# A feed-forward block: the next block's transposes put ahead of the last row tile, and the router's softmax put eight groups behind its matmuls

## The reference

```python
x = x + layernorm(attention(layernorm(x), W_qkv, W_out))
x = x + layernorm(ffn(layernorm(x), router_w, w1, b1, w2, b2))

def ffn(x, router_w, w1, b1, w2, b2):
    xt = x.reshape(-1, H)                                 # H = 1024, F = 4096
    p = softmax(matmul(xt, router_w))                     # 8 experts
    top, idx = top_k(p, 2)
    top = top / sum(top)
    combine = einsum('tk,tke->te', top, one_hot(idx, 8))
    out = matmul(gelu(matmul(xt, w1) + b1), w2) + b2
    return out * sum(combine, axis=-1, keepdims=True)
```

## Time and profile before

| what | value |
|---|---|
| profiled execution, device time | 1846.83 us |
| its span (slowest core, core 6) | 1845.3 us |
| spans of the eight cores | 1804.3 to 1845.3 us |
| mean granted TensorE clock of the cores | 0.902 to 0.924 |
| runs listed | 1857.76 and 1940.99 us, median 1899.37 us |
| TensorE busy | 1445.2 us, 78% of the span |

### The profile page before, as it was taken

How to read it: one execution, slowest core, us unless ns; L and a number is a source line. 1 busy time by engine, 2 the same in 40 slices (tenths; PEclk the granted TensorE clock), 3 DMA queues, 4 the chain that set the end, 5 groups by cost and what they waited for, 6 DMA issues and landing times.

```text
span 1845.3 us, 19508 instructions; the slowest of 8 cores (1804.3 to 1845.3 us)
## 1 busy us (share of the span) xinstructions
PE 1445.2 (78%) x6816; PEld 648.8 (35%) x6816; DVE 594.8 (32%) x1102; ACT 558.7 (30%) x1181; POOL 57.9 (3%) x101
## 2 busy tenths in 40 slices
PE   0588777888788788878878888873897897897897
PEld 0233333333334333333333333331343343343343
DVE  0443444543233333333333333332213213214103
ACT  0402110220132233323333333334353353353333
POOL 1000000000000000000000000101000000000000
PEclk9989999899998888888888988887898898998898
DMA  9312201110400111111100001878703002102002
GB/s 137 64 29 46 46 12 35 23 23 1 86 7 1 29 29 29 29 29 28 22 24 26 19 28 29 125 143 144 119 24 83 10 24 70 22 13 79 1 1 80
DMA packets 51617, 81.55 MB, mean 44 GB/s; under 512 B 19648, under 2 KB 27840, under 8 KB 51520
## 3 DMA queue, kind: packets, MB, share of 16 engines
q0 software_dynamic: 27280, 50.35, 16.7%
q1 hardware_dynamic: 24240, 29.94, 5.3%
HBM read 97.08 MB, written 20.97 MB: 64 GB/s over the span
## 4 chain that ended last, share of the span: by engine, by line
PE 65%; DVE 13%; DMA 10%; issue 6%; ACT 3%; SPq 1%; DVEq 0%; POOL 0%; ACTq 0%; POOLq 0%
PE pAll L185 31%; PE pAll L160 31%; DMA qtile<-qs 5%; DMA xgb<-xo 3%; DVE ptb L750 2%; PE pAll L216 2%; DMA qs<-qstage 2%; DVE vt L496 2%; DVE xfg L439 1%; DVE sm L374 1%; DVE m L677 1%; DVE x2t L832 1%; DMA x2lt<-x2s 1%; DVE qstage L467 1%; PE pAll L1061 1%
## 5 line engine op out<-in xcount | busy, mean ns | idle before, releaser
L160 PE MATMUL pAll<-kf,qtile 128*128 128x512 bf16 x1024 | 256.8, 411 | 35.5 <-DMA qtile<-qs 32.1
L160 PE MATMUL pAll<-x2f,w1b 128*128 128x512 bf16 x1024 | 237.8, 396 | 24.3 <-ACT h1g L1162 20.1
L185 PE MATMUL pAll<-vt,ptb 128*128 128x512 bf16 x1024 | 226.4, 382 | 0.9 <-DVE ptb L750 0.9
L185 PE MATMUL pAll<-w2b,h1g 128*128 128x512 bf16 x1024 | 221.7, 379 | 4.1 <-ACT h1g L1162 4.1
L677 DVE TENSOR_REDUCE m<-pAll 128x1 f32<-128x512 f32 x128 | 88.5, 692 | 353.5 <-PE pAll L160 353.2
L160 PEld LDWEIGHTS pAll<-kf,qtile 128*128 128x128 bf16 x1024 | 106.0, 105 | 177.6 <-issue 80.2
L688 ACT ACTIVATE pbuf<-pAll,nb 128x512 bf16<-128x512 f32 x128 | 87.8, 686 | 261.1 <-DVE nb L682 261.1
L160 PEld LDWEIGHTS pAll<-x2f,w1b 128*128 128x128 bf16 x1024 | 102.9, 101 | 157.2 <-issue 47.7
L185 PEld LDWEIGHTS pAll<-vt,ptb 128*128 128x128 bf16 x1024 | 100.8, 98 | 123.9 <-issue 4.8
L185 PEld LDWEIGHTS pAll<-w2b,h1g 128*128 128x128 bf16 x1024 | 99.9, 98 | 125.9 <-issue 6.0
L185 PE MATMUL pAll<-wvb,xfg 128*128 128x512 bf16 x512 | 115.6, 379 | 35.5 <-DVE vt L496 35.5
(11 more groups left out here) (109 smaller groups left out, 1032.2 us busy)
## 6 DMA issues: line engine op xcount, KB each, us to landing
xrt<-xo POOLq DMA_DIRECT2D x16, 512.0 KB, 7.8
x2s<-x2t SPq DMA_DIRECT2D x16, 512.0 KB, 3.7
w1b<-w POOLq DMA_DIRECT2D x8, 1024.0 KB, 32.1
w2b<-w POOLq DMA_DIRECT2D x4, 2048.0 KB, 45.0
x2rt<-x2s SPq DMA_DIRECT2D x16, 512.0 KB, 5.3
y<-yt SPq DMA_DIRECT2D x16, 512.0 KB, 3.3
xgb<-xo POOLq DMA_DIRECT2D x16, 256.0 KB, 8.4
qs<-qstage POOLq DMA_DIRECT2D x16, 256.0 KB, 2.7
```

The source lines that it names most:

```text
L160: return e.matmul(o(), l(), r(), start=st, stop=sp)
L185: return e.matmul(o(), l(), r(), start=st, stop=sp)
```

## The change

`c_pass2` is cut in two. `c_pass2_mm`, behind fc = 6, keeps the router's matmuls and the four copies to `rt8`. `c_pass2_chain`, behind fc = 14, has the rest: maximum, Exp and the steps to `sc4`, tile after tile as before. And `c_pass1(gc + 1)` is called behind the epilogue of k = 2 instead of behind that of k = 3. What is computed stays the same. The lines behind L1084 are numbered differently in the changed kernel: L1100 is L1102, L1112 to L1140 are L1120 to L1148, L1162 is L1170, L1195 is L1205, L1208 is L1218, L1217 is L1227.

```diff
-    def c_pass2(gc):
+    ev_rtcp = {}
+
+    def c_pass2_mm(gc):
         for t in range(4):
-            qt = gc * 4 + t
             bank = rt_banks[t % 2]
...
             mm_group(bank, mms, waits=list(ev_x2f_evac[(gc, t)]) + [ev_rw])
             r8 = rt8[:, t * 8:(t + 1) * 8]
             wrt = list(rt_slice_prev.get(t, ()))
-            ev_rt = read_bank("scalar", [bank],
-                              lambda e, d=r8, b=bank: e.copy(d, b.ap[:, 0:8]),
-                              waits=wrt, inc="sS")
+            ev_rtcp[(gc, t)] = read_bank(
+                "scalar", [bank],
+                lambda e, d=r8, b=bank: e.copy(d, b.ap[:, 0:8]),
+                waits=wrt, inc="sS")
+
+    def c_pass2_chain(gc):
+        for t in range(4):
+            qt = gc * 4 + t
+            r8 = rt8[:, t * 8:(t + 1) * 8]
+            ev_rt = ev_rtcp[(gc, t)]
             mxr = rsm[:, 0:1]
...
             if fc == 6:
-                c_pass2(gc)
+                c_pass2_mm(gc)
+            elif fc == 14:
+                c_pass2_chain(gc)
         cx2f_free[0] = E.ev("tS")
...
-        if gc + 1 < 4:
-            c_pass1(gc + 1)
+            if k == 2 and gc + 1 < 4:
+                c_pass1(gc + 1)
```

## The result

The changed kernel took 1870.4 us (median of 11 runs), the kernel before 1847.1 (median of 10); the ratio is 1.0134, 95% interval 1.0088 to 1.0180. It is slower, by 1.3%.

A forecast was written before the change was run, and what follows sets the result against it. TensorE, busy for 78% of the span, was taken as the bound. The profiled 1846.8 us plus 21.7 for the move of c_pass1 and 2.8 for the router split gave 1871.3, stated as 1871 us; range 1857 to 1892.

The forecast's parts named there:

- the price of the clock: Lower granted clock slows matmuls behind each new GELU wait ahead of group 3: 2.7 us lost, bounds 0 and 2.9.
- The boundary: From copy of k = 2 to the next block's fourth up-projection group: 41.15 us against 36.6, so 4.55 later.
- The move alone: Moving c_pass1 behind k = 2's epilogue costs 7.2 us at each of three block boundaries, +21.7 (13.6 to 22.4).
- The router: Splitting the router pass: chain as long as before, router fills now outside it; +0.7 us four times, +2.8 (0 to 4).
- No cost at k = 3: The 64 matmuls of k = 3 behind c_pass1 run at full rate, 13.8 us; at half rate 13.8 more each.
- A clock that stays up: Rival: clock does not fall ahead of group 3 or behind the wait at fc = 14; 1847 us, chance 0.05.
- Longer table switches: Rival: seven new ScalarE table switches behind busy work last longer than their load; 1876 us, chance 0.08.
- The two others: Rivals: k = 3 stays at lower clock, 1912 us, 0.05; casts overtake the epilogue at boundaries, 1841 us, 0.02.
- within 2%: Whole kernel's time changes by less than about 2%, here 37 us; chance 0.89, slower by more 0.09, faster 0.02.

The follow-up runs named there:

- experiments 1 to 3: Stage (before 563.2 us): 1, split only 566.9, move only 580.9; 2, changed kernel, casts ahead of k = 2's epilogue, 553.2; 3, six up-projection banks, changed 546.4, before 535.8.
- Experiment 4: Changed kernel with matmuls whose result nothing reads, filling TensorE's GELU waits ahead of groups 3 and 18; stage 573.9 us against 585.7 for the changed kernel.
- experiment 7: Scratch columns per router tile, four Exp one behind the other: on the changed kernel, stage 541.5 us; on the kernel of experiment 6, 480.8.
- 504.8 kernel: Kernel before, router pass whole, with c_pass1 between matmuls and epilogue of k = 2 and six up-projection banks; stage 504.8 us against 563.2.
- experiment 6: 504.8 kernel with the four router fills in one bank, one copy of 32 columns, and seven up-projection banks; stage 502.4 us.

## Where the prediction was right, and the step that failed

The mechanism was right: each wait that was forecast appears where it was forecast, and the change costs 22.5 us for a forecast of 24.5. **The step that failed is the price of the clock.** I took 2.7 us lost behind each of the three new waits, 8.1 of the sum; they measured 2.9, 1.4 and 1.7, 5.9 together. I had taken the slow matmuls behind one wait as the price of every such wait. The rows show no fixed price: behind waits of 4.49, 4.19 and 4.19 us TensorE ran at 0.50 for 5.9, 2.7 and 3.3 us. It is the same at the router: I took 2.9 lost for each block, before and after, and it was 2.6, 2.9, 1.8 and 2.7 in the kernel before, 2.2, 1.8, 2.7 and 1.6 in the changed one. What sets how long the clock stays down is not shown by these runs.

The sum, term by term, as the mean of the six cores (0, 1, 3, 5, 6 and 7) whose two traces have every matmul of the two projections on record:

| term | forecast, us | measured, us |
|---|---|---|
| from the copy of k = 2 to the fourth group, three boundaries | +13.65 | +14.5 |
| slow matmuls behind the new wait, three boundaries | +8.1 | +5.85 |
| from group 7 to the end of the up-projection, four blocks | +2.8 | +2.0 |
| the last down-projection | 0 | +0.3 |
| sum | +24.5 | +22.6 |

**The boundary.** Right by its steps. Forecast from the copy of k = 2 at the last boundary: resumption 10.75, measured 1701.56 - 1690.80 = 10.76; fills 5.6, measured 5.15, where the clock came back earlier (5.57 at the two others); k = 3 13.8 plus 0.26, measured 14.07 from its first matmul to its copy; then 10.75 to group 3, measured 10.69. Together 41.15 forecast, 1731.47 - 1690.80 = 40.67 measured, and 41.1 as the mean of all boundaries. Before, I had taken 36.6 for each; the mean is 36.3, so the delay is 4.8 and not 4.55. That the new wait is ScalarE's, behind the epilogue of k = 3, and not VectorE's or the fills', is shown by experiments 1 to 3: it comes with the move, stays when the casts go first, and goes with banks.

**The move alone.** It measured +17.7 where the prediction had +21.7. The clock behind the new waits is 2.0 of these 4 us (6.1 lost in place of 8.1). The other 2.0 were gained behind the router, where the prediction had put nothing: 1.7 us are lost behind its waits in blocks 1 to 3, where the kernel before lost 2.9, 1.8 and 2.7. (The waits themselves are 3.4 us shorter in all, but groups 7 to 9 ahead of them are slower by about as much.) Experiment 4 shows that what is lost behind a wait is the clock.

**The router.** Four times +0.7, 2.8 us, measured 3.2 to 3.7 alone and 2.0 in the changed kernel. Right in mechanism: the chain keeps its length and the router's fills stand outside it. What I called the round trips of the chain is shown by experiment 7.

**No cost at k = 3.** I took no loss there between bounds of 0 and 13.8. Measured: 14.20, 14.22 and 13.98 for the 64 matmuls at the three boundaries, against 13.97 at full rate: 0 to 0.25.

**The rivals.** A clock that stays up: at the last boundary it was 1.00 where group 3 started, which this rival needs and which I had named as a sign of being wrong, but it fell about 1 us later, and the matmuls behind paid all the same. Longer table switches: L1218 ends at 1729.32 and the load starts at 1729.34, GELU 14 ends at 1459.14 and the load starts at 1459.16, and in both places the next instruction follows 1.3 us later. The drain of some 1380 ns that the Trainium skill (ScalarE: Activation LUTs, section "What ACT_TABLE_LOAD costs") adds to a switch does not show in these rows. The two others did not occur.

**The level and what can be told.** The time, 1871 forecast and 1870.4 measured, agrees better than the sum that it was built from, and that is in part luck. The sum stood on one execution, 1846.8, which happens to lie at the level of the runs taken later, median 1847.1; both runs listed beside it lay higher, and against their median, 1899, the same 1871 would have read as faster. I also gave most of the chance to "within 2%" and called 2% about what a measurement can tell from no change. That step was wrong as well: the interval is half a per cent to either side of 1.0134 and excludes 1.

## What to carry to other kernels

Before a piece of work is moved ahead of a tile, look at what the queues hold in front of its helpers on the other engines: moved from behind one epilogue to behind another, it takes its wait along, and the epilogue it no longer hides appears in the next consumer. A wait that TensorE has for ScalarE is shortened by what shortens ScalarE's absence or by more banks to run ahead in, not by moving the absence; splitting a chain of round trips leaves the round trips. Price a TensorE wait with the slow matmuls behind it, here 1.4 to 2.9 us on top of 4, and 1.6 to 2.7 on top of 9; take it as a range, not as one value.

## What was not expected

The clock fell behind short pauses as well. In the 504.8 kernel TensorE paused 1.25 and 2.05 us for router copies, with eight small matmuls between (stretches of core 0; length, PE busy, clock, DMA share, GB/s):

```profile
1403.00:1405.00 2.00, 0.24 (x9) 0.73 0.00 0
1405.00:1407.00 2.00, 2.00 (x10) 0.50 0.04 8
...
1411.00:1414.00 3.00, 3.00 (x15) 1.00 0.00 0
```

Without the pauses (experiment 6) the same small matmuls left it at 1.00 for the 7 us behind them, so it was the pauses and not the small matmuls.

In the run with filled waits, cores 6 and 7 had a granted clock of 0.81 through most of the first up-projection, while the other six had 1.00 in the same part of the program (core 7; same columns):

```profile
1300.00:1320.00 20.00, 19.40 (x104) 0.81 1.08 168
...
1350.00:1380.00 30.00, 28.64 (x134) 1.00 0.00 1
```

This is what put their stage 9 to 10 us above the others'. The same two cores had 0.81 early in the stage with the split alone (until 1291 us) and with six banks in the changed kernel (until 1331 us). Why these two cores, and why then, stays open; no run was made for it.
